# First-norm scale and bias moved from VectorE to ScalarE, and the first product of FF1 issued in one piece

## The reference

```python
def _block(x, p):                                   # 8 times, by lax.scan
    residual = x
    q, k, v = x @ Wq + bq, x @ Wk + bk, x @ Wv + bv
    Q, K = elu(q) + 1.0, elu(k) + 1.0
    KV = einsum('nsh,nsh->nh', K, v); Ksum = sum(K, axis=1)
    V = Q * KV[:, None, :] / (Q * Ksum[:, None, :] + EPS_Z)
    x = _layernorm(gelu(V @ Wo + bo) + residual, ln1_s, ln1_b)
    residual = x
    h = gelu(x @ Wf1 + bf1)                         # 128 -> 512
    ff = gelu(h @ Wf2 + bf2)                        # 512 -> 128
    return _layernorm(ff + residual, ln2_s, ln2_b)

x = x + ga * attn_stack(_layernorm(x) * (1 + ca) + sa)
x = x + gb * mixture_of_experts(_layernorm(x) * (1 + cb) + sb)
```

## Time and profile before

| | |
|---|---|
| time, 3 executions | 579.0 us median (578.59 to 581.25) |
| profiled execution: span from first to last instruction | 579.1 us |
| mean granted TensorE clock | 0.988 |
| PE busy | 528.0 us (91%) |
| DVE busy | 488.8 us (84%) |
| ACT busy | 392.8 us (68%) |
| POOL busy | 251.5 us (43%) |
| the 31 gelus `g2` (one each slot, 3 to 33) | start 45.22 us to 442.87 us |

### The profile page before, as it was taken

One profiled execution on the slowest core, in us unless ns is written; L12 is line 12 of the kernel. 1 busy time (PEld: TensorE's weight loads), 2 busy tenths in 40 slices (PEclk: granted clock), 3 DMA queues, 4 the chain that ended last, 5 costly groups with the idle time before them and its releaser, 6 DMA issues.

```text
span 579.1 us, 7876 instructions
## 1 busy us (share of the span) xinstructions
PE 528.0 (91%) x1892; PEld 296.1 (51%) x1892; DVE 488.8 (84%) x1747; ACT 392.8 (68%) x564; POOL 251.5 (43%) x217
## 2 busy tenths in 40 slices
PE   3789999999999999899999999989978999999997
PEld 2345445555555554555555555545545334766664
DVE  5759998999999999999999999998997666988764
ACT  2657777777777777777777777777765635464641
POOL 2234454444444445444444444444443233555542
PEclk9989999999999999999999999999998999999999
DMA  8100010001000000100010000001000000000000
GB/s 254 51 0 16 5 38 0 14 5 36 14 5 9 28 14 5 36 0 14 5 36 14 5 18 18 14 5 36 1 1 1 0 2 1 0 19 2 18 13 25
DMA packets 15909, 11.21 MB, mean 19 GB/s; under 512 B 8188, under 2 KB 13692, under 8 KB 15892
## 3 DMA queue, kind: packets, MB, share of 16 engines
q1 hardware_dynamic: 15316, 10.42, 6.5%
q10 hardware_dynamic: 576, 0.60, 0.3%
HBM read 9.96 MB, written 1.05 MB: 19 GB/s over the span
## 4 chain that ended last, share of the span: by engine, by line
DVE 42%; PE 25%; POOL 16%; issue 13%; DMA 1%; ACT 1%; DVEq 0%; POOLq 0%; SPq 0%
DVE xhD L817 7%; POOL rsD L723 6%; DVE xhB L817 5%; POOL rsB L723 5%; PE bank L283 5%; DVE mq L886 4%; DVE kk L889 4%; POOL qq L739 3%; DVE elu_q_sb L893 3%; DVE stD L794 3%; DVE x L857 3%; PE bank L465 3%; PE bank L467 3%; DVE vt L864 3%; DVE stB L794 2%
## 5 line engine op out<-in xcount | busy, mean ns | idle before, releaser
L368 PE MATMUL bank<-hid,wf 128*128 128x512 f32 x256 | 125.6, 592 | 0.0
L723 POOL TENSOR_TENSOR rsD<-veD,c_half 128x4 f32<-128x4 f32 x32 | 38.6, 1205 | 134.0 <-DVE veD L807 134.0
L359 PE MATMUL bank<-x,wf 128*128 128x512 f32 x192 | 94.1, 599 | 0.0
L635 ACT ACTIVATE hid<-bank,vbf 128x512 f32<-128x512 f32 x128 | 81.0, 689 | 7.8 <-PE bank L359 3.9
L368 PEld LDWEIGHTS bank<-hid,wf 128*128 128x128 f32 x256 | 46.0, 190 | 46.0 <-issue 29.9
L739 POOL TENSOR_TENSOR qq<-elu_q_sb,ones 128x512 f32<-128x512 f32 x32 | 40.5, 1267 | 53.8 <-DVE elu_q_sb L893 53.8
L736 POOL TENSOR_TENSOR y<-g,xs 128x512 f32<-128x512 f32 x32 | 40.8, 1276 | 36.5 <-ACT g L641 36.5
L684 ACT ACTIVATE sg<-bank 128x512 f32<-128x512 f32 x40 | 23.9, 598 | 46.8 <-PE bank L469 35.0
L359 PEld LDWEIGHTS bank<-x,wf 128*128 128x128 f32 x192 | 37.3, 194 | 33.3 <-issue 24.7
L784 POOL TENSOR_TENSOR sc_lo<-sc,sc_hi 128x512 fp32r<-128x512 f32 x28 | 36.4, 1302 | 39.6 <-ACT sc_hi L692 36.2
L817 DVE TENSOR_SCALAR xhD<-bank,meanD,rsD 128x128 f32<-128x128 f32 x128 | 43.8, 404 | 8.3 <-POOL rsD L723 8.3
(11 more groups left out here) (149 smaller groups left out, 1195.4 us busy)
## 6 DMA issues: line engine op xcount, KB each, us to landing
wf<-in_w_f SPq DMA_DIRECT2D x16, 256.0 KB, 2.6
wu<-in_w_unit SPq DMA_DIRECT2D x10, 192.0 KB
wqkv<-in_w_qkv SPq DMA_DIRECT2D x7, 192.0 KB, 2.3
x<-in_x SPq DMA_DIRECT2D x4, 256.0 KB, 6.8
out<-ot SPq DMA_DIRECT2D x4, 256.0 KB, 2.7
wo<-in_w_o SPq DMA_DIRECT2D x8, 64.0 KB, 1.8
wmod<-in_w_mod ACTq DMA_DIRECT2D x1, 384.0 KB, 3.8
vln<-in_v_ln SPq DMA_DIRECT2D x16, 1.0 KB, 1.7
```

The lines of the kernel that those rows point to most:

```text
L359: mm = nc.tensor.matmul(ps_ff[j][:], wf1[:, j * P:(j + 1) * P], x2[(c - 2) % CH][:], start=True, stop=True)
L368: mm = nc.tensor.matmul(ps_f0[:], wf2[:, j, :], hid[:, j, :], start=(j == 0), stop=(j == FJ - 1))
L635: nc.scalar.activation(hid[:, j, :], ps_ff[j][:], ACT.Gelu_apprx_tanh, bias=vbf1[:, j:j + 1]).then_inc(h_ready, 1)
L723: nc.gpsimd.tensor_tensor(rs[buf(k, n)][:], ve[buf(k, n)][:], c_half[:], ALU.pow).then_inc(rstd_ready[k], 1)
```

## The change

`x2` of an item is no longer written by DVE at the head of its slot in two halves, but by ACT in one operation, an Identity activation with a scale and a bias from SBUF. It stands in ACT's list after `dd` and ahead of `ek`. `ff1(0)` becomes one product of 512 columns like the three others. `x2_ready` now counts one for each item. The list of POOL stays.

```diff
@@ SP, layer_loads
-                    sp.wait_ge(x2_ready, HB * CH * l)
+                    sp.wait_ge(x2_ready, CH * l)
                 sp.dma_start(vln1[:], v_ln1[l]).then_inc(ld["vln1"], 16)
@@ PE, ff1(j)
                     if j == 0:
 
-                        for h in range(HB):
-                            pe.wait_ge(x2_ready, HB * f + h + 1)
-                            mm = nc.tensor.matmul(half(ps_ff[0], h), wf1[:, 0:P], half(x2[(c - 2) % CH], h),
-                                                  start=True, stop=True)
-                    else:
-                        mm = nc.tensor.matmul(ps_ff[j][:], wf1[:, j * P:(j + 1) * P], x2[(c - 2) % CH][:],
-                                              start=True, stop=True)
-                    mm.then_inc(ff1_mm, 1)
+                        pe.wait_ge(x2_ready, f + 1)
+                    nc.tensor.matmul(ps_ff[j][:], wf1[:, j * P:(j + 1) * P], x2[(c - 2) % CH][:],
+                                     start=True, stop=True).then_inc(ff1_mm, 1)
@@ PE, ahead of the product with wo
-                    wait(pe, x2_ready, HB * b)
+                    wait(pe, x2_ready, b)
@@ ACT, slot
                     nc.scalar.activation(dd[:], lden[:], ACT.Exp, bias=c_lneps[:, 0:1], scale=-1.0).then_inc(dd_ready, 1)
+                if has(f):
+                    act.wait_ge(to_fm["B"], f + 1)
+                    if (c - 2) % CH == 0:
+                        act.wait_ge(ld["vln1"], 4 * f + 16)
+                    nc.scalar.activation(x2[(c - 2) % CH][:], ps_b[:], ACT.Identity,
+                                         bias=vln1[:, 1:2], scale=vln1[:, 0:1]).then_inc(x2_ready, 1)
                 if has(a):
                     act.wait_ge(k_mm, a + 1)
@@ DVE, slot
-                if has(f):
-                    dve.wait_ge(to_fm["B"], f + 1)
-                    if (c - 2) % CH == 0:
-                        dve.wait_ge(ld["vln1"], 4 * f + 16)
-                    for h in range(HB):
-                        nc.vector.tensor_scalar(half(x2[(c - 2) % CH], h), half(ps_b, h), vln1[:, 0:1], vln1[:, 1:2],
-                                                ALU.mult, ALU.add).then_inc(x2_ready, 1)
                 if has(b):
```

More of the change, by code:

```diff
@@ L489, in up @@
                 if i == 0:
-                    pe.wait_ge(x2_ready, HB * NI)
+                    pe.wait_ge(x2_ready, NI)
                 if i == 1:
```

## The result

The changed kernel takes 591.8 us (median of 4, 591.13 to 591.9), the kernel before 578.8 us (median of 4, 577.5 to 581.25) on the same chip: ratio 1.0223, 95% interval 1.0188 to 1.0257. It is 13.0 us slower; 590.5 was forecast, with 586.5 to 595.5.

What follows compares the result with a forecast made beforehand. DVE's list was taken as the limit, replaced after the change by a loop over ACT's list of 13.50 us against 13.18. Terms 9.0 + 0.8 + 0.2 + 1.5 = +11.5 on 579.1 gave 590.5 us, range 586.5 to 595.5.

Steps and rivals of the forecast that it cites:

- What bounded the old kernel: DVE's list, with its few waits, was taken as the loop closing last: 12.07 us busy in a 13.2 us slot.
- The loop over ACT's list: From `g2` over `x2` and `ff1(1)` to the next `g2`: 13.50 us against 13.18, chance 0.81.
- the release: From the end of `x2` to PE's weight load for `ff1(0)`: 0.05 us.
- What hides: `ek` to `hid` 0 move back about 0.69 us, PE by 0.32; ACT's 1.01 us idle before `g1` covers the 0.37 difference.
- The port: Rival: DVE's `mq`, started ahead of POOL's `y1`, delays `y1`; about 0.25 us a slot, 598 us, chance 0.07.
- The clock in the loop: Rival: PE's wait before `ff1(0)` lowers its clock; each `ff1(0)` at half clock gives 616 us, chance 0.04.
- slot 32, "0": In slot 32 ACT would have `x2` done before PE starts FF1 at 432.42, so no difference.
- slot 33, "+1.5": In slot 33 `x2` stands behind `ex`, so `ff1(1)` starts 0.8 to 1.7 us later by clock level; +1.5 taken.
- The turns of the loop: Extra time at the loop's turns, mean period 0.03 us above the clean 13.18; if it recurs, +0.8 us.
- The base: The +11.5 us was added to the profiled 579.1 us, with the median, 579.0, called the same base.
- No change: Rival: DVE's gain in slots where it is late gives back the new loop's cost; 579 us, chance 0.04.
- faster: Rival: with ACT not in the loop, PE and DVE go at a 12.61 us period; 563 us, chance 0.04.

Runs made afterwards that it cites:

- early `mq`: Kernel before, with DVE's `mq` moved directly behind `elu_k_sb`, ahead of `xhD`: 562.6 us, ratio 0.9726.
- spare copies: Changed kernel with one spare 128x256 copy on ACT to a scratch tile: ahead of `x2` 600.4 us, directly behind `x2` 590.9 us.
- the last `x2` first: Changed kernel with `x2` of slot 33 alone put ahead of the router's exponential and its table load: 587.5 us, ratio 1.0153.

## Why the prediction was right, point by point

- **What bounded the old kernel.** Right, and more exactly than I had put it first: not DVE's sum of work, but the loop in which `mq` is held by `y1`. The early `mq` took 15.5 us from the kernel before with no work removed; in the slot looked at, 0.41 of the 0.47 us won on DVE's list is the hold that is gone.
- **The loop over ACT's list.** Right in its course and to 0.04 us in its sum, 13.50 against 13.54. Its terms measured: `g2` to `x2` 3.76 (forecast 3.76); `x2` 0.76 (0.78); end to load 224.90 to 225.01, 0.11 (0.05); load to `ff1(1)` 0.96 (0.97); `ff1(1)` to `g2` 7.95 (7.94). The one term mis-sized is the release, taken from the row of DVE's second half; behind a whole piece it is 0.11 us on either engine (last section). The spare copies show that this list is the path, and only its part ahead of `x2`.
- **What hides.** Right: idle before `g1` 0.70 (0.6 or 0.7 forecast), before `g2` 0.94 (0.94), PE's wait for `x2` 34.8 us (some 35), DVE's for `dd` 1.7 us a slot (1 to 2).
- **The port.** Right as weighed: `mq` came 0.23 us ahead of `y1` (forecast 0.24), and `y1` took 1.32 us instead of 1.28, so nothing of it reached PE.
- **The clock in the loop.** It stayed up, so that rival fell. At the end it did not stay put, and two terms were mis-sized by it: slot 32, "0", was -1.6 us, since FF1 there ran at the lower level before and at full clock after; slot 33, "+1.5", was +2.8: 1.4 by the later start of FF1 (5.11 us behind `g2` for 3.75) and 1.4 since all three products of FF1 and the transposes behind them ran at the lower level. That the two errors nearly cancel is luck. The mechanism named for slot 33, `x2` behind `ex`, is shown by moving it: 4.3 us back by the medians, 4.2 in the traces.
- **The turns of the loop.** Every fourth period was 13.61, 0.08 more: 0.6 us over the whole, for 0.8 forecast.
- **The base.** "The span and the median can be read as one" was wrong: the time of an execution is some 2 us above its span, and the profiled execution of before, with a span of 579.1, was some 2.3 us slower than the median one. So the forecast of +11.5 us stands between 10.7 by the spans and 13.0 by the medians; that 590.5 comes within 1.3 us of 591.8 owes something to luck. The period, +0.32 forecast and +0.35 measured, doesn't.
- **No change, faster.** Neither came. DVE was given 51 us and the loop had no place for them.

## What to carry to other kernels

When work is moved off the busiest engine, don't ask how busy the receiver is; write down the closed loop that the moved operation joins there, from its result back to its own predecessor in the list, and add its rows. Here that took five rows and gave the period to 0.3%. A DVE and a POOL operation that hold each other up can set the period of a whole pipeline (`mq`: 0.42 us alone, 0.83 to 1.32 under `y1`): look for an instruction that takes twice its usual time, and move it before moving any work. And pieces that look like overhead (two halves) may be what lets the next engine start early.

## What the runs showed of the hardware that I had not expected

- A DVE operation from SBUF to SBUF also holds POOL: the power `rsD` takes 1.02 us alone (slot 32), 1.21 to 1.28 in the loop, where `mk` runs at its start, and 1.49 (median) with `mk` and then `mq` in its way in the early-`mq` kernel. It is not so for every pair: `y1` grew by only 0.04 us where `mq` had started 0.23 us ahead of it.
- The release from the end of `x2` to PE's weight load goes by the form and not by the engine. Behind the second half it was 0.05 us, on DVE (220.98 to 221.03) and on ACT (223.95 to 224.00, `x2` and `ff1(0)` in halves); behind a whole piece 0.11 us, on ACT (224.90 to 225.01) and on DVE (223.01 to 223.12, before with `x2` whole). Why is not shown. The loads of ACT's second half and of DVE's whole piece:

```profile
224.00 0.30 PEld L356 LDWEIGHTS bank<-x,wf 128*128 128x128 f32 x2 [0.16 <-ACT x L628]
```

```profile
223.12 0.30 PEld L355 LDWEIGHTS bank<-x,wf 128*128 128x128 f32 x2 [0.34 <-issue]
```

- At the seam to the second part, with a pause of 1.53 us ahead of it, FF1 took 5.46 us at 0.50 granted clock; with 0.17 us of pause 2.81 us at 1.00. But the pause alone doesn't decide. In the kernel before the clock fell in the same place with no pause directly ahead of `ff1(0)`, after waits of 0.60 and 0.92 us with work between; the run with the last `x2` first has these two waits as well (0.60 and 0.91) and stays at 1.00. In slot 32 of the kernel before it fell at about 432.3, 1.7 us behind the end of a wait of 2.99; in the changed one it stayed at 1.00 through waits of 2.07 and 0.74. In the loop, a pause of 1.1 us each slot never lowered it. What makes the difference at the seam no run here shows.
